# Banded attention weights built on TensorE from sixteen diagonal blocks, and tanh written over its own input

## The chip, the cores and the metric

The kernel runs on all 8 cores of one Trainium2 chip. Every core runs the same program on its own batch element (2048 tokens of width 1024); nothing passes between the cores. The metric is the device time in microseconds of the slowest core.

## The reference

For each of 8 batch elements, `x` is `[2048, 1024]` in f32, and two layers follow, each with a layer norm ahead of it, a layer norm behind it, and a residual:

```python
xn     = layernorm(x)
q      = xn @ w1
proj   = pad(xn) @ w2                         # 7 zero rows ahead, 8 behind
score[t, k] = tanh(proj[t + k] + q[t]) @ v    # k = 0..15
weight = softmax(score, axis=-1)              # 16 weights per token
out[t] = sum_k weight[t, k] * pad(xn)[t + k]
x      = x + layernorm(out)

h      = layernorm(x)                          # mixture of 8 experts, top 2, and one shared
y      = sum_e cw[e] * (silu(h @ wg[e]) * (h @ wu[e])) @ wd[e] + shared(h)
x      = x + layernorm(y)
```

The change lies in the first layer alone.

## The kernel before, in words

Every engine has one list of operations, written in program order by `P.add(engine, fn, waits, inc)`. An engine works through its list strictly in that order; an operation waits for the semaphore values named in `waits`, and `inc` raises a semaphore when it is done. So the order in which the Python code calls `P.add` sets the order of work on each engine.

**The attention layer.** 16 tiles of 128 tokens are taken in 4 stages (`sp`) of 4 tiles (512 tokens).

- `emit_windows_qproj(sp)` copies the last part of the window along, transposes the new tiles of `xn` on TensorE into `xnw` (`ptw`, L300 and L308), then computes q (8 groups of 8 matmuls into `pq`, L320, each evicted to `qw` by VectorE, L329) and the local projection (8 groups of 8+8 matmuls into `pq` and `ptf`, L339 and L346, evicted to `pjw`, L356 and L359). `pq` has two banks.
- `emit_scores_softmax(sp)` is a loop of 32 steps (16 offsets k times two halves of the width). Each step is: four VectorE additions into one of two buffers `argb[i]` (L388, 128x512 each), one tanh on ScalarE of the whole 128x2048 buffer into `tanb[i]` (L394), and four matmuls with `vsp` that add the result into 16 rows of one PSUM bank `psc` (L403). The additions wait for the tanh that read this `argb[i]` two steps ago; the tanh waits for the matmuls that read this `tanb[i]` two steps ago. Behind the loop come a copy of the scores (L414), a burst of 12 matmuls on `idb` and `argb` whose result nobody reads (`warm_burst`, L604), four small transposes (L419) and the softmax into `wts`.
- `make_tail(sp, ev_wt)` gives a list of thunks that finish the stage: for each of the 4 tiles `t_ub` builds `uwide`, a 128x384 band matrix with `weight[t, k]` on diagonal `121 + k`; `t_band_tr` transposes its two or three 128x128 pieces on TensorE (`ptb`, L490) and copies them to `wtb` (L499); `t_band` multiplies them with `xn` into the two banks `pB` (L514); `t_stats` takes the statistics (L534) and moves `pB` to `bbuf` (L550). Behind the four tiles come one `t_rstd` and four `t_x2`, which normalise (ScalarE, L568) and add to `x2` (VectorE, L577).

The thunks of stage `sp` are pumped one by one into the code of stage `sp+1`: one after each window transpose, q group and projection group, and what is left after each step of the score loop. The thunks of the last stage have nothing beside them. So 12 of the 16 calls of `t_ub` stand between transposes and projection groups of the next stage, and 4 stand alone.

`t_ub` before is VectorE work only: one memset of `uwide` (L464) and 16 `scalar_tensor_tensor` operations (L470), each adding `idb * wts[:, k]` to a shifted 128x128 piece of `uwide`. Since neighbouring pieces overlap, each waits (`drain`) until the one ahead of it has been written.

**The expert layer** (from L610 on) waits for all of the attention layer: its weight loads on the GpSimd queue wait for `bar`, the last semaphore values of TensorE, VectorE and ScalarE, and its matmuls need the finished `x2`. It is not touched.

**Start.** Constants and `w1`, `w2` are loaded by the GpSimd queue in the order `idb`, `onesb`, `vsp`, `wrt`, `w1s`, `w2s`.

Of the kernel before, what the change touches and what calls it, by code (L numbers as in the profile page):

```python
# [10 lines left out]
BF16 = mybir.dt.bfloat16  # L11
# [5 lines left out]
KW = 16  # L17
# [66 lines left out]
def build_program(cfg: Cfg):  # L84
    nc = bass.Bass("TRN2", target_bir_lowering=False)
# [15 lines left out]
    d_iw = nc.dram_tensor("iw", [128, 448], F32, kind="ExternalInput").ap()  # L101
# [4 lines left out]
    with ExitStack() as ctx:  # L106
        en = ctx.enter_context
# [4 lines left out]
        P = Prog(sems)  # L112

        x2 = en(nc.sbuf_tensor("x2", [128, TT * H], F32))
        idf = en(nc.sbuf_tensor("idf", [128, 128], F32))
        idb = en(nc.sbuf_tensor("idb", [128, 128], BF16))
        onesb = en(nc.sbuf_tensor("onesb", [128, 128], BF16))
        vsp = en(nc.sbuf_tensor("vspb", [128, HC * KW * KW], BF16))
# [11 lines left out]
        for q in range(4):  # L130
# [3 lines left out]
                out=x2[:, lo * H: hi * H],  # L134
                in_=d_x.rearrange("(tt p) h -> p tt h", p=128)[:, lo:hi, :]),
                inc=f"dx{q}", inc_amt=16))
        ev_x = ev_xq[-1]
        ev_id = P.add("sync", lambda e: e.dma_start(out=idf[:], in_=d_id),
                      inc="dc", inc_amt=16)
        P.add("gpsimd", lambda e: e.dma_start(out=idb[:], in_=d_id),  # L140
              inc="dgc", inc_amt=16)
        P.add("gpsimd", lambda e: e.dma_start(out=onesb[:], in_=d_ones),
              inc="dgc", inc_amt=16)
        P.add("gpsimd", lambda e: e.dma_start(
            out=vsp[:], in_=d_vsp.rearrange("(c p) j -> p c j", p=128)),
            inc="dgc", inc_amt=16)
        ev_const = P.add("gpsimd", lambda e: e.dma_start(
            out=wrt[:], in_=d_wrt.rearrange("(c p) j -> p c j", p=128)),
            inc="dgc", inc_amt=16)
        ev_iw = ev_idb = ev_onesb = ev_vsp = ev_wrt = ev_const  # L150
# [34 lines left out]
        with ExitStack() as actx:  # L185
            aen = actx.enter_context
# [5 lines left out]
            pjw = aen(nc.sbuf_tensor("pjw", [128, HC * 768], BF16))  # L192
            GW = min(4, HC)
            argb = [aen(nc.sbuf_tensor(f"argb{i}", [128, GW * 512], BF16)) for i in range(2)]
            tanb = [aen(nc.sbuf_tensor(f"tanb{i}", [128, GW * 512], BF16)) for i in range(2)]
            scf = aen(nc.sbuf_tensor("scf", [16, 512], F32))
            sct = aen(nc.sbuf_tensor("sct", [128, 64], F32))
            wts = aen(nc.sbuf_tensor("wts", [128, 4 * KW], F32))
            uwide = [aen(nc.sbuf_tensor(f"uwide{i}", [128, 384], BF16)) for i in range(2)]
# [8 lines left out]
            pB = [aen(nc.psum_tensor(f"pB{i}", [128, 512], F32)) for i in range(2)]  # L208

            P.add("gpsimd", lambda e: e.dma_start(  # L210
                out=w1s[:], in_=d_w1.rearrange("(c p) j -> p c j", p=128)),
                inc="dw", inc_amt=16)
            ev_w2 = P.add("gpsimd", lambda e: e.dma_start(
                out=w2s[:], in_=d_w2.rearrange("(c p) j -> p c j", p=128)),
                inc="dw", inc_amt=16)
# [9 lines left out]
            for tau in range(TT):  # L225
# [4 lines left out]
                    waits=[ev_a1], inc="s")  # L230
# [7 lines left out]
            ev_pB_free = [None, None]  # L238
            ev_sc_prev = None
            argb_free = [None, None]  # L240
            tanb_free = [None, None]
            uw_free = [None, None]
# [2 lines left out]
            ev_s_sct = None  # L245
            ev_s_smx = None
            ev_s_bbuf = None
            zscr_free = [None]
            ev_q = ev_pj = None
            ev_sctv = None  # L250
# [117 lines left out]
            def emit_scores_softmax(sp, pump=None):  # L368
                nonlocal ev_sc_prev, ev_s_sct, ev_s_smx, ev_sctv, ev_tf_last
                ev_q_sp, ev_pj_sp = ev_q, ev_pj  # L370
# [10 lines left out]
                for k in range(KW):  # L381
                    for cq in range(HC // GW):
                        i = nq % 2
                        eva = None
                        for ci in range(GW):
                            c = cq * GW + ci
                            eva = P.add("vector", lambda e, k=k, c=c, ci=ci, i=i:
                                        e.tensor_tensor(  # L388
                                argb[i][:, ci * 512:(ci + 1) * 512],
                                pjw[:, c * 768 + 121 + k: c * 768 + 121 + k + 512],  # L390
                                qw[:, c * 512:(c + 1) * 512], op=A.add),
                                waits=[ev_q_sp, ev_pj_sp, argb_free[i]],
                                inc="v" if ci == GW - 1 else None)
                        evth = P.add("scalar", lambda e, i=i: e.activation(  # L394
                            tanb[i][:], argb[i][:], AF.Tanh),
                            waits=[eva, tanb_free[i]], inc="s")
                        argb_free[i] = evth
                        for ci in range(GW):
                            c = cq * GW + ci
                            ev_sc = P.add("tensor", lambda e, k=k, c=c, ci=ci, i=i,  # L400
                                          first=(nq == 0 and ci == 0),
                                          last=(nq == NQ - 1 and ci == GW - 1):
                                          e.matmul(  # L403
                                psc[0:16, 0:512],
                                vsp[:, c * KW * KW + k * KW:
                                    c * KW * KW + (k + 1) * KW],
                                tanb[i][:, ci * 512:(ci + 1) * 512],
                                start=first, stop=last),
                                waits=[evth, ev_vsp, ev_sc_prev],
                                inc="t" if ci == GW - 1 else None)  # L410
                        tanb_free[i] = ev_sc
                        nq += 1
                        spp(1)
# [4 lines left out]
                for blk in range(4):  # L418
# [3 lines left out]
                        waits=[ev_scev, ev_id, ev_tf_last, ev_ptf_tail], inc="t")  # L422
# [13 lines left out]
                for blk in range(4):  # L436
# [5 lines left out]
                        waits=[evn], inc="s")  # L442
# [5 lines left out]
                ev_wt = None  # L448
# [8 lines left out]
            def make_tail(sp, ev_wt):  # L457
                b0 = sp * 4
                state = {"ev_v2": None, "ev_bev": [None] * 4}

                def t_ub(blk, ui):
                    def f():
                        def ub(e, blk=blk, ui=ui):
                            e.memset(uwide[ui][:], 0.0)  # L464
                            last = None
                            for k in range(KW):
                                off = k + 121
                                wcol = wts[:, blk * KW + k: blk * KW + k + 1]
                                e.drain()
                                last = e.scalar_tensor_tensor(  # L470
                                    uwide[ui][:, off: off + 128], idb[:], wcol,
                                    uwide[ui][:, off: off + 128],
                                    op0=A.mult, op1=A.add)
                            return last
                        state[f"ub{blk}"] = P.add(
                            "vector", ub, waits=[ev_wt, ev_idb, uw_free[ui]],
                            inc="v")
                        P.drain("vector")
                    return f

                def t_band_tr(blk, tau, kaps, ui):
# [104 lines left out]
                for blk in range(4):  # L586
                    tau = b0 + blk
                    kaps = [kp for kp in (tau - 1, tau, tau + 1) if 0 <= kp < TT]
                    ui = blk % 2
# [26 lines left out]
            for sp in range(NSP):  # L616
                ev_wt = emit_scores_softmax(sp, pump=tail)
# [10 lines left out]
        with ExitStack() as mctx:  # L628
# [226 lines left out]
            for th in range(2):  # L855
# [6 lines left out]
                for ei in range(NE):  # L862
# [6 lines left out]
                    for ic in range(IC):  # L869
                        sl = nload % 3  # L870
                        gn, un = gname[ic % 2], uname[ic % 2]
                        gb, ub = pbank[gn], pbank[un]
# [266 lines left out]
```

How the kernel before makes its waits and increments, by code:

```python
            def body(eng):  # L68
                for fn, wl, inc in ops[engname]:
                    for semname, val in wl:
                        eng.wait_ge(sems[semname], val)
                    if fn is None:
                        continue
                    inst = fn(eng)
                    if inc is not None:
                        inst.then_inc(sems[inc[0]], inc[1])
```

## Time and profile before

| what | us |
|---|---|
| median of the runs before (2 runs, 3165.08 and 3167.39) | 3166.24 |
| the profiled execution, its own time | 3169.17 |
| span of its slowest core (core 5), first to last instruction | 3167.4 |
| spans of the 8 cores | 3153.4 to 3167.4 |
| attention layer on core 5, to the last addition to `x2` | 0 to 816.7 |
| expert layer on core 5 | 816.7 to 3167.4 |

The span is what the trace shows; the execution's own time holds 1.8 us more around it. Rows of the trace are in us from the start of the span. A timeline row is: start, duration, engine, line, operation, what it writes and reads, how many instructions are merged, and in brackets how long the engine stood idle before it and who released it. TensorE's matmuls are pipelined and their ends are modelled. "PEclk" is the clock that TensorE was granted: 1.00 is 2.4 GHz, 0.50 is 1.2 GHz.

### The profile page before, as it was taken

The numbers are of one execution on the slowest core, as the hardware profiler recorded it, in microseconds if no ns is written. First come the engines' busy times: TensorE is split into PE (matmuls) and PEld (weight loads), VectorE is DVE, ScalarE is ACT, GpSimd is POOL, SyncE is SP. The second block draws the span as 40 slices with busy tenths as digits, with TensorE's granted clock in tenths as the row PEclk, the third lists the DMA queues.
The fourth block names the chain that finished last, engine by engine and source line by source line (L and its number), as shares of the span: only waits on it lengthen the run. The fifth ranks groups of instructions, "written<-read, shape, count | busy, mean of one in ns | idle before, by whom it ended". The sixth has DMA issues, their size and how long they took to land.

```text
span 3167.4 us, 31804 instructions; the slowest of 8 cores (3153.4 to 3167.4 us)
## 1 busy us (share of the span) xinstructions
PE 2518.9 (80%) x11570; PEld 1122.3 (35%) x11570; DVE 1213.6 (38%) x2370; ACT 539.8 (17%) x485; POOL 505.3 (16%) x550
## 2 busy tenths in 40 slices
PE   2654554633267999999999999599999999999995
PEld 1221221201123444444444444244444444444442
DVE  5564655556434233233233222522222232222225
ACT  2522517053211111101111101010010010010010
POOL 0000000000012222212212312022222222222220
PEclk9986887767579999999999999699999999999997
DMA  7000000000247776966966967478768778769763
GB/s 168 1 0 1 1 1 1 1 0 0 20 39 71 67 66 63 92 62 64 90 62 64 91 65 68 83 67 83 73 65 83 73 66 84 72 65 86 73 65 72
DMA packets 626055, 179.41 MB, mean 57 GB/s; under 512 B 618608, under 2 KB 619760, under 8 KB 625904
## 3 DMA queue, kind: packets, MB, share of 16 engines
q0 software_dynamic: 621344, 160.55, 53.9%
q1 hardware_dynamic: 4560, 16.84, 1.5%
q8 instruction: 95, 1.56, 0.2%
q14 instruction: 56, 0.46, 0.1%
HBM read 329.48 MB, written 8.39 MB: 107 GB/s over the span
## 4 chain that ended last, share of the span: by engine, by line
PE 72%; DVE 14%; ACT 8%; issue 3%; DVEq 2%; DMA 2%; ACTq 0%; POOLq 0%
PE py L983 21%; PE pg L893 12%; PE pu L909 12%; PE py L909 10%; PE py L893 10%; ACT tanb L394 6%; DVE uwide L470 3%; PE pq L320 2%; PE pq L339 1%; DVE bnb L154 1%; DVEq L62 1%; DVE argb L388 1%; PE psc L403 1%; DMA wdb<-wd 1%; PE pB L514 1%
## 5 line engine op out<-in xcount | busy, mean ns | idle before, releaser
L983 PE MATMUL py<-hpr,wdb 128*128 128x512 bf16 x3168 | 713.4, 387 | 48.4 <-DVE hpr L932 40.1
L983 PEld LDWEIGHTS py<-hpr,wdb 128*128 128x128 bf16 x3168 | 312.8, 100 | 438.4 <-issue 88.7
L893 PE MATMUL pg<-xm_fm,wgb 128*128 128x512 bf16 x1728 | 395.1, 382 | 3.0 <-DVE cwb L841 3.0
L909 PE MATMUL pu<-xm_fm,wub 128*128 128x512 bf16 x1728 | 390.6, 379 | 0.0
L879 POOL DMA_DIRECT2D wgb<-wg x176 | 156.2, 887 | 1400.3 <-DVE x L577 810.9
L924 DVE TENSOR_TENSOR t1b<-sgb,pu 128x1024 bf16<-128x1024 bf16 x108 | 131.9, 1221 | 527.4 <-PE pu L909 527.4
L1001 DVE SCALAR_TENSOR_TENSOR yfm<-py,yfm 128x1024 f32<-128x1024 f32 x128 | 156.8, 1225 | 456.7 <-PE py L983 447.9
L909 PE MATMUL py<-xm_fm,wub 128*128 128x512 bf16 x1440 | 325.5, 379 | 0.0
L893 PE MATMUL py<-xm_fm,wgb 128*128 128x512 bf16 x1440 | 325.5, 379 | 0.0
L403 PE MATMUL psc<-tanb,vspb 128*16 128x512 bf16 x512 | 155.7, 434 | 188.3 <-ACT tanb L394 188.3
L394 ACT ACTIVATE tanb<-argb 128x2048 bf16<-128x2048 bf16 x128 | 233.8, 1897 | 330.7 <-DVE argb L388 308.6
L920 ACT ACTIVATE sgb<-pg 128x1024 bf16<-128x1024 f32 x108 | 110.6, 1024 | 991.2 <-PE pg L893 991.1
L924 DVE TENSOR_TENSOR t1b<-sgb,py 128x1024 bf16<-128x1024 bf16 x90 | 109.9, 1221 | 436.7 <-PE py L909 436.7
L893 PEld LDWEIGHTS pg<-xm_fm,wgb 128*128 128x128 bf16 x1728 | 170.0, 98 | 210.3 <-issue 9.4
L909 PEld LDWEIGHTS pu<-xm_fm,wub 128*128 128x128 bf16 x1728 | 169.1, 98 | 203.9
L883 POOL DMA_DIRECT2D wub<-wu x176 | 155.7, 884 | 331.8 <-PE py L909 166.5
L893 PEld LDWEIGHTS py<-xm_fm,wgb 128*128 128x128 bf16 x1440 | 140.9, 98 | 169.9
L909 PEld LDWEIGHTS py<-xm_fm,wub 128*128 128x128 bf16 x1440 | 140.9, 98 | 169.9
L388 DVE TENSOR_TENSOR argb<-pjw,qw 128x512 bf16<-128x512 bf16 x512 | 182.6, 420 | 45.2 <-ACT tanb L394 42.3
L973 POOL DMA_DIRECT2D wdb<-wd x80 | 84.8, 1060 | 686.0 <-PE pg L833 383.6
L920 ACT ACTIVATE sgb<-py 128x1024 bf16<-128x1024 f32 x90 | 92.2, 1024 | 520.7 <-PE py L893 520.7
L403 PEld LDWEIGHTS psc<-tanb,vspb 128*16 128x16 bf16 x512 | 40.7, 93 | 300.9 <-issue 275.9
(119 smaller groups left out, 1318.8 us busy)
## 6 DMA issues: line engine op xcount, KB each, us to landing
wgb<-wg POOLq DMA_DIRECT2D x176, 256.0 KB, 5.3
wub<-wu POOLq DMA_DIRECT2D x176, 256.0 KB, 5.3
wdb<-wd POOLq DMA_DIRECT2D x128, 352.0 KB, 6.6
x<-x SPq DMA_DIRECT2D x4, 2048.0 KB, 24.3
out<-osc SPq DMA_DIRECT2D x16, 512.0 KB, 2.6
wgb<-wgs POOLq DMA_DIRECT2D x22, 256.0 KB, 4.9
wub<-wus POOLq DMA_DIRECT2D x22, 256.0 KB, 5.3
wdb<-wds POOLq DMA_DIRECT2D x16, 352.0 KB, 6.3
```

What stands on the lines that cost most here:

```text
L388: e.tensor_tensor(argb[i][:, ci * 512:(ci + 1) * 512], pjw[:, c * 768 + 121 + k: c * 768 + 121 + k + 512], qw[:, c * 512:(c + 1) * 512], o ...
L394: evth = P.add("scalar", lambda e, i=i: e.activation(tanb[i][:], argb[i][:], AF.Tanh), waits=[eva, tanb_free[i]], inc="s")
L403: e.matmul(psc[0:16, 0:512], vsp[:, c * KW * KW + k * KW: c * KW * KW + (k + 1) * KW], tanb[i][:, ci * 512:(ci + 1) * 512], start=first, s ...
L470: last = e.scalar_tensor_tensor(uwide[ui][:, off: off + 128], idb[:], wcol, uwide[ui][:, off: off + 128], op0=A.mult, op1=A.add)
L879: evlg_ = P.add("gpsimd", lambda e, sl=sl, src_g=src_g: e.dma_start(out=wgb[sl][:], in_=src_g.rearrange("(c p) j -> p c j", p=128)), waits ...
L883: evlu_ = P.add("gpsimd", lambda e, sl=sl, src_u=src_u: e.dma_start(out=wub[sl][:], in_=src_u.rearrange("(c p) j -> p c j", p=128)), waits ...
L893: last = e.matmul(gb[:, gg * 512:(gg + 1) * 512], wgb[sl][:, c * 128:(c + 1) * 128], xm_fm[:, c * T + tof + gg * 512: c * T + tof + (gg + ...
L909: last = e.matmul(ub[:, gg * 512:(gg + 1) * 512], wub[sl][:, c * 128:(c + 1) * 128], xm_fm[:, c * T + tof + gg * 512: c * T + tof + (gg + ...
L920: evsg = P.add("scalar", lambda e, gb=gb: e.activation(sgb[:], gb[:, 0:TH], AF.Silu), waits=[evg, ev_sgb_cons], inc="s")
L924: evt1 = P.add("vector", lambda e, ub=ub: e.tensor_tensor(t1b[:], sgb[:], ub[:, 0:TH], op=A.mult), waits=[evsg, evu, ev_t1b_cons], inc="v")
L983: last = e.matmul(pbank[pyn][:, gg * 512:(gg + 1) * 512], wdb[sl][:, ic * 128:(ic + 1) * 128], hpr[:, ic * TH + gg * 512: ic * TH + (gg + ...
L1001: e.scalar_tensor_tensor(yfm[:, c * TH:(c + 1) * TH], pbank[pyn][:, 0:TH], 1.0, yfm[:, c * TH:(c + 1) * TH], op0=A.mult, op1=A.add),
```

## The change

Two things are changed, both in the attention layer.

1. `tanb` becomes another name for `argb`: the tanh writes over its own input. The additions of a step therefore wait for two things: the tanh that used the buffer two steps ago, as before, and the four matmuls that read its result.
2. `t_ub` no longer adds up the band on VectorE. VectorE writes 16 separate diagonal blocks into a new buffer `DallA` (128x2048), TensorE multiplies each with a shifted piece of a constant `iwb` (448 columns, ones on diagonal `p + 160`) and adds all 16 products up in `pB[0]`, and VectorE copies 384 columns from there to `uwide`. `pB[0]` has to be free before (the copy to `bbuf` of the tile ahead), and `DallA` too (the matmuls of the tile ahead). One more constant load, `iwb`, stands first in the GpSimd queue.

```diff
+        iwb = en(nc.sbuf_tensor("iwb", [128, 448], BF16))
...
+        P.add("gpsimd", lambda e: e.dma_start(out=iwb[:], in_=d_iw),
+              inc="dgc", inc_amt=16)
         P.add("gpsimd", lambda e: e.dma_start(out=idb[:], in_=d_id),
               inc="dgc", inc_amt=16)
...
-            tanb = [aen(nc.sbuf_tensor(f"tanb{i}", [128, GW * 512], BF16)) for i in range(2)]
+            tanb = argb
+            DallA = aen(nc.sbuf_tensor("DallA", [128, KW * 128], BF16))
...
-                                waits=[ev_q_sp, ev_pj_sp, argb_free[i]],
+                                waits=[ev_q_sp, ev_pj_sp, argb_free[i],
+                                       tanb_free[i]],
                                 inc="v" if ci == GW - 1 else None)
...
-                        def ub(e, blk=blk, ui=ui):
-                            e.memset(uwide[ui][:], 0.0)
+                        nonlocal ev_dallA_free
+
+                        def dbuild(e, blk=blk):
                             last = None
                             for k in range(KW):
-                                off = k + 121
                                 wcol = wts[:, blk * KW + k: blk * KW + k + 1]
-                                e.drain()
-                                last = e.scalar_tensor_tensor(
-                                    uwide[ui][:, off: off + 128], idb[:], wcol,
-                                    uwide[ui][:, off: off + 128],
-                                    op0=A.mult, op1=A.add)
+                                last = e.tensor_scalar(
+                                    DallA[:, k * 128:(k + 1) * 128], idb[:],
+                                    wcol, None, op0=A.mult)
                             return last
-                        state[f"ub{blk}"] = P.add(
-                            "vector", ub, waits=[ev_wt, ev_idb, uw_free[ui]],
-                            inc="v")
+                        evd = P.add("vector", dbuild,
+                                    waits=[ev_wt, ev_idb, ev_dallA_free],
+                                    inc="v")
                         P.drain("vector")
+
+                        def ummA(e):
+                            last = None
+                            for k in range(KW):
+                                s0_ = 39 - k
+                                last = e.matmul(
+                                    pB[0][:, 0:384],
+                                    DallA[:, k * 128:(k + 1) * 128],
+                                    iwb[:, s0_: s0_ + 384],
+                                    start=(k == 0), stop=(k == KW - 1))
+                            return last
+                        evm = P.add("tensor", ummA,
+                                    waits=[evd, ev_iw, ev_pB_free[0]], inc="t")
+                        ev_dallA_free = evm
+                        ev = P.add("vector", lambda e, ui=ui: e.tensor_copy(
+                            uwide[ui][:], pB[0][:, 0:384]),
+                            waits=[evm, uw_free[ui]], inc="v")
+                        ev_pB_free[0] = ev
+                        state[f"ub{blk}"] = ev
```

On TensorE, in the q projection of the second stage around its second tile, the program before has these rows (`pq` with `w1s` is a q group, `ptb` the transposes of the band, `pB` its product with `xn`):

```order
L320 MATMUL pq<-xnw,w1s 128x512 x24
L490 MATMUL ptb<-idb,uwide 128x128 x3
L320 MATMUL pq<-xnw,w1s 128x512 x8
L514 MATMUL pB<-xn,wtb 128x512 x2
L320 MATMUL pq<-xnw,w1s 128x512 x8
```

and the changed program these (its line numbers are higher by 5 to 23):

```order
L325 MATMUL pq<-xnw,w1s 128x512 x16
L488 MATMUL pB<-iwb,DallA 128x384 x16
L325 MATMUL pq<-xnw,w1s 128x512 x8
L513 MATMUL ptb<-idb,uwide 128x128 x3
L325 MATMUL pq<-xnw,w1s 128x512 x8
L537 MATMUL pB<-xn,wtb 128x512 x2
```

The 16 new matmuls stand one q group ahead of the transposes, so the third group of eight that used to stand ahead of the tile's TensorE work now stands behind the new matmuls.

On VectorE at the same place, before (`qw` is the eviction of a q group):

```order
L550 COPY bbuf<-pB 128x512 x2
L329 CAST qw<-pq 128x512
L464 MEMSET uwide 128x384
L470 SCALAR_TENSOR_TENSOR uwide<-idb,wts,uwide 128x128 x16
L329 CAST qw<-pq 128x512
L499 COPY wtb<-ptb 128x384
```

and in the changed program:

```order
L573 COPY bbuf<-pB 128x512 x2
L334 CAST qw<-pq 128x512
L475 TENSOR_SCALAR DallA<-idb,wts 128x128 x16
L497 CAST uwide<-pB 128x384
L334 CAST qw<-pq 128x512
L522 COPY wtb<-ptb 128x384
```

The copy of `uwide`, which waits for TensorE, stands directly behind the 16 products, ahead of the next eviction.

On VectorE at the third step of the score loop of the first stage, before and then in the changed program (what an operation waits for in brackets, s is ScalarE's semaphore, t TensorE's):

```order
L388 TENSOR_TENSOR argb<-pjw,qw 128x512 [waits s]
```

```order
L393 TENSOR_TENSOR argb<-pjw,qw 128x512 [waits s,t]
```

The additions of a step now wait for TensorE too.

## Rows read from the trace of the kernel before

**Rows 1.** The page's chain that ended last: share of the span by engine.

```profile
PE 72%; DVE 14%; ACT 8%; issue 3%; DVEq 2%; DMA 2%; ACTq 0%; POOLq 0%
```

**Rows 2.** Stretches: length, busy of PE, PEld, DVE, ACT, POOL (count), PEclk, DMA, GB/s.

```profile
118.70:177.00 58.30, 33.24 (x124) 9.39 (x124) 42.93 (x120) 57.81 (x32) 0.00 (x0) 0.95 0.00 1
319.05:362.90 43.85, 25.61 (x92) 7.11 (x92) 32.68 (x92) 43.44 (x24) 0.00 (x0) 0.92 0.00 0
504.33:546.30 41.97, 24.13 (x88) 6.71 (x88) 31.25 (x88) 41.62 (x23) 0.00 (x0) 0.93 0.00 1
695.37:735.50 40.13, 23.13 (x84) 6.42 (x84) 29.81 (x84) 39.82 (x22) 0.00 (x0) 0.92 0.00 1
```

**Rows 3.** Timeline, score loop of the first stage: tanh, matmuls and additions of one step.

```profile
122.82 54.11 ACT L394 ACTIVATE tanb<-argb 128x2048 bf16<-128x2048 bf16 x30 [0.42 <-PE psc L403]
...
126.67 1.02 PE L403 MATMUL psc<-tanb,vspb 128*16 128x512 bf16 x4 [0.78 <-ACT tanb L394]
128.43 1.43 DVE L388 TENSOR_TENSOR argb<-pjw,qw 128x512 bf16<-128x512 bf16 x4 [0.37 <-ACT tanb L394]
```

**Rows 4.** Timeline, one step of the second stage's loop with a `t_x2` beside it.

```profile
299.35 1.43 DVE L388 TENSOR_TENSOR argb<-pjw,qw 128x512 bf16<-128x512 bf16 x4
300.93 1.91 ACT L394 ACTIVATE tanb<-argb 128x2048 bf16<-128x2048 bf16 x1 [3.00 <-DVE argb L388]
...
302.98 1.87 PE L403 MATMUL psc<-tanb,vspb 128*16 128x512 bf16 x4 [4.17 <-ACT tanb L394]
...
305.39 1.43 DVE L388 TENSOR_TENSOR argb<-pjw,qw 128x512 bf16<-128x512 bf16 x4
```

**Rows 5.** Timeline, end of the first score loop: last matmuls, copy, burst.

```profile
177.07 1.02 PE L403 MATMUL psc<-tanb,vspb 128*16 128x512 bf16 x4 [0.78 <-ACT tanb L394]
178.20 0.68 DVE L414 COPY scf<-psc 16x512 f32<-16x512 f32 x1 [3.34 <-PE psc L403]
...
179.03 2.75 PE L604 MATMUL psc<-argb,idb 128*128 128x512 bf16 x12 [0.93 <-DVE scf L414]
```

**Rows 6.** Granted clock: a stretch (columns as in rows 2), then timeline rows of matmuls.

```profile
288.00:320.00 32.00, 9.33 (x20) 1.98 (x20) 13.67 (x31) 17.54 (x13) 0.00 (x0) 0.50 0.00 1
```

```profile
256.38 1.89 PE L339 MATMUL pq<-xnw,w2s 128*128 128x512 bf16 x8 [1.14 <-DVE pjw L359]
...
260.76 3.17 PE L339 MATMUL pq<-xnw,w2s 128*128 128x512 bf16 x8 [2.04 <-DVE pjw L359]
```

**Rows 7.** Timeline, start of the third stage's loop: third tanh.

```profile
462.75 1.91 ACT L394 ACTIVATE tanb<-argb 128x2048 bf16<-128x2048 bf16 x1 [0.42 <-PE psc L403]
```

**Rows 8.** Groups by form, 0 to 1100 us: count, busy, mean ns, idle before.

```profile
L470 DVE SCALAR_TENSOR_TENSOR uwide<-idb,wts,uwide 128x128 bf16<-128x128 bf16 x256 | 90.4, 353 | 20.1 <-issue 1.4
...
L329 DVE CAST qw<-pq 128x512 bf16<-128x512 f32 x32 | 22.1, 692 | 43.9 <-PE pq L320 40.3 <-PE pB L514 2.5 <-issue 1.1
...
L359 DVE CAST pjw<-ptf 128x128 bf16<-128x128 f32 x32 | 9.0, 280 | 0.0
```

**Rows 9.** Timeline, expert layer: eight products of `idb` with one column.

```profile
898.76 1.39 DVE L817 TENSOR_SCALAR Dsc<-idb,cw_all 128x128 bf16<-128x128 bf16 x8 [0.17 <-DVE cw_all L778]
```

**Rows 10.** Timeline, second tile's `t_ub` in the second stage's q projection.

```profile
209.69 0.38 DVE L464 MEMSET uwide<- 128x384 bf16 x1
210.14 6.77 DVE L470 SCALAR_TENSOR_TENSOR uwide<-idb,wts,uwide 128x128 bf16<-128x128 bf16 x16
...
217.05 0.48 PE L490 MATMUL ptb<-idb,uwide 128*128 128x128 bf16 x3 [8.92 <-DVE uwide L470]
...
217.32 3.34 PE L320 MATMUL pq<-xnw,w1s 128*128 128x512 bf16 x8
```

**Rows 11.** Timeline, last stage's tail, second tile: the band's product on TensorE.

```profile
768.20 2.72 PE L514 MATMUL pB<-xn,wtb 128*128 128x512 bf16 x6 [0.61 <-DVE wtb L499]
```

**Rows 12.** DMA issues, 0 to 300 us: KB, us to landing; and the first user of the weights.

```profile
w2s<-w POOLq DMA_DIRECT2D x1, 2048.0 KB, 58.3
```

```profile
71.60 1.87 PE L320 MATMUL pq<-xnw,w1s 128*128 128x512 bf16 x4 [0.94 <-DVE xnw L308]
```

More of the change, by code:

```diff
@@ L247, in build_program @@
             ev_s_bbuf = None
+            ev_dallA_free = None
             zscr_free = [None]
```

## Prediction

> **What bounds the kernel now.** I read the views from the whole to the place. The chain that ended last [rows 1] is 72% TensorE; that is the expert layer, which the change does not touch and which starts only when the attention layer is complete. So whatever the attention layer gains or loses is passed on one to one: the weight loads of the expert layer wait for its end too. Inside the attention layer two stretches matter.
>
> The first is the score loop. In the table of stretches [rows 2] I cut out the parts of the four loops in which nothing else is mixed in: 32, 24, 23 and 22 tanh in 58.3, 43.9, 42.0 and 40.1 us, 101 of the 128 steps. In each of the four rows ScalarE is busy for 99% of the stretch. The timeline [rows 3] gives the beat: 30 tanh in 54.11 us, 1.80 us each; the four matmuls take 1.02 and then idle 0.78, the additions take 1.43 and idle 0.37. ScalarE sets the end; the two others have room. The other 27 steps have tail work beside them and a longer beat (299.35 to 305.39 is 6.04 us [rows 4]).
>
> The second is `t_ub`, 16 times. In the second tile of the second stage [rows 10] VectorE works from 209.69 to 216.91 (7.22 us), and TensorE stands still for 8.92 us before the transposes of the band at 217.05.
>
> **The tanh in place.** The buffer of a step may be rewritten only when its matmuls are done. Before, additions and matmuls of neighbouring steps lay beside each other; now one buffer goes round a closed circle, and there are two buffers. The circle from rows: additions 1.43; to the tanh 0.15 (300.78 to 300.93); tanh 1.91; to the matmuls 0.14 (302.84 to 302.98) [rows 4]; matmuls; from their end back to VectorE 0.11 (178.09 to 178.20) [rows 5]. Without the matmuls that is 3.74. The matmuls take 1.02 at full clock [rows 3] and 1.87 at half clock [rows 4]. So a circle is 4.76 or 5.61 us and carries two steps, which took 3.60 before: 1.16 or 2.01 us more per pair. The third and every later step of a stretch waits this way: 15, 11, 11 and 10 circles in the stretches of 32, 24, 23 and 22, 47 in all. That gives +54.5 us at full clock and +94.5 at half clock. The loosely filled steps (6.04 apart, matmuls done 0.54 before the next additions [rows 4]) have slack and cost nothing.
>
> Which clock? In the loop before, the matmuls are busy 57% with gaps of 0.78 and the clock in rows 2 is 0.92 to 0.95 (the first matmuls of each are slow, the rest fast). In the stretch 288 to 320 they are busy 29% and the clock is 0.50 throughout [rows 6]. The new loop at full clock would be busy 43% and has gaps of 0.78 and 1.94 in turn, between the two. A gap of 2.04 us was enough once: eight matmuls took 1.89 at 256.38 and 3.17 at 260.76 behind that gap [rows 6]. And once the clock is lost the new loop is busy 1.87 of 2.80 us, with gaps, where the rises in this trace came out of almost unbroken work. I take three quarters of the way to half clock: +84.5.
>
> The Trainium skill ("TensorE: Matmul & The Clock Gate", § HAM oscillation — how this bites in real kernels) ties the loss of the clock to long idle gaps only, longer than any in the new loop; by that the loop would stay at full clock. The same page's § A second HAM failure mode: psum-queue depth-cycling says that short idles between groups of matmuls make the clock swing between both levels, which is nearer to my mix. The gap of 2.04 us agrees with the second. No row shows 43%.
>
> Two small terms go with it. If the loop ends at half clock, the burst of 12 matmuls, 2.75 us at full clock [rows 5] and ahead of the score transposes on TensorE, takes up to 5.3: I take +1.5 for each of four, +6 (0 to +10). And at the start of the third and fourth loop the third additions, which before were written ahead so that only the tanh waited for TensorE, at 462.75 [rows 7], wait for it themselves; additions and hand-over (1.43+0.15) then stand between: +1.5 each, +3 (0 to +4).
>
> **The band on TensorE.** Removed: 7.22 us of VectorE per tile, 16 x 353 ns plus drains [rows 8] and a memset. Added on VectorE: 16 products like those of L817. Eight take 1.39 us [rows 9], so sixteen at most 2.78. Then 0.13 to TensorE. 16 matmuls of 384 columns are as many columns as 12 of 512: 2.75 us at full clock [rows 5], and with 0.427 us per 512 columns (eight in 3.57 or 3.34, the rows at half clock) 5.28 at half. TensorE has stood idle there for most of the 8.92 us of before [rows 10] and starts at half clock; the rise comes during or just behind them: I take 4.9. Then 0.11, and the copy of 384 columns from PSUM: between 280 ns for 128 and 692 for 512 [rows 8] that is 555 ns, and 0.12 on. Together 2.78+0.13+4.9+0.11+0.56 = 8.48 against 7.22: +1.26 per tile (-0.9 to +1.6). VectorE is free for longer but can't use it: the copy of `uwide` stands directly behind the products, and the next evictions behind it.
>
> For the 12 tiles among projections two things come on top. One group of eight matmuls (1.9, with the 128-column ones 2.3) that used to run while VectorE was busy now stands behind the new matmuls, with the 0.67 of the copy hidden beside it: +1.6. And what follows runs at full clock, 1.7 instead of 3.34 at 217.32 [rows 10]: -1.6. So +1.26 per tile, +15 in all. Bounds: every new matmul at full clock and the gain kept, -0.9 per tile, -11; all at half clock and no gain, +3.2, +38. For the four tiles of the last stage the six matmuls behind, 2.72 at 768.20 [rows 11], fall to about 1.45: -1.3 against +1.26, so 0 (-6 to +6).
>
> The new constant load costs nothing: `w2s` lands about 64 us (issued at 5.4, 58.3 on the way [rows 12]), its first user starts at 71.60 behind VectorE's copies. The extra load moves 0.2 MB ahead of it and some 0.9 us of issue; the cover is 7 us.
>
> **Sum.** +84.5 + 6 + 3 + 15 + 0 = +108.5 us, 3.4%. On the profiled execution's 3169.2 that is 3277.7; the median of the runs is 2.9 lower, so 3275.
>
> **The rivals.**
> - *The loop keeps full clock.* +54.5, burst 0, starts +3, band about +10: +67, 3234. For it: gaps of 0.78 to 1.94 are shorter than most idles after which the clock was gone. Against it: 43% busy and the 2.04 gap. Its lower bound, with the band at -11, is 3210.
> - *The lost clock is everywhere.* +94.5, burst +10, starts +4, band +38, tail +6: +152.5, 3319. For it: TensorE is idle ahead of every group in the attention layer. Against it: the 16 new matmuls are the kind of unbroken work after which the clock rose.
> - *The band pays for the loop.* VectorE saves 7.22 - 3.34 = 3.88 us per tile, 62 us in 16. If all of that came off the path while the loop kept full clock, 54.5 - 62 = -7.5: 3159, not slower. It decides from the point where TensorE's 16 matmuls are hidden beside VectorE work, so that only 3.3 us per tile are left on the path. Against it: 2.75 us is their least, and the copy behind them is next in VectorE's order.
> - *The new wait never binds*, because the matmuls are done when the additions come up. The trace excludes it: the additions at 128.43 start before the matmuls of the tanh for which they wait, at 126.67 + 1.80 = 128.47, which then last 1.02 [rows 3].
>
> **How the numbers follow.** My forecast 0.58, full clock in the loop 0.22, half clock everywhere 0.16, band pays 0.04. A measurement of this kernel tells about 2% (63 us) from no change. The border is 3229.6; below it lie the third rival and the lower part of the first: within 2% 0.17, faster 0.02, slower 0.81. The range 3222 to 3312 reaches from the lower middle of the first rival to just short of the second.
>
> **What would show it right or wrong.** In the changed profile: the beat of the tanh in the unmixed loops 2.4 to 2.8 instead of 1.80, VectorE idle before the additions and released by the matmuls, ScalarE busy about 70% there; the granted clock there tells which circle it is. The 16 products 2.7 us together, the 16 new matmuls 2.8 to 5.3, the copy 0.55. The four stages start later by 25 to 35 us each, and the expert layer has the same length as before. A beat of 1.80 would prove the main step wrong; a beat right and a total under 3220 would mean that the band gains what I hold for hidden.

## The result, and the profile after

The changed kernel takes 3.5% longer: ratio of the runs 1.0353, 95% interval 1.0337 to 1.0368, that is 112 us on 3166; the forecast was 109. Its profiled execution took 3277.57 us with a span of 3275.1 on the slowest core (core 3). These comparisons leave out executions in which the cores of a die ran at a lower clock and the time is longer whatever the kernel; the plain medians over all runs (3279.88 and 3256.6) mix them in and say little, and where some cores of a profiled execution below still show it, the others are given as well.

Where it lies shows best at the moment of the first weight load of the expert layer, which waits for the whole attention layer. Averaged over the 8 cores it stands at 816.3 us in the kernel before and at 925.8 in the changed one, +109.5; from there to the end it is 2344.1 and 2344.7 us. The expert layer passes the loss on and adds nothing. The average over the cores is used below as "the attention layer", since single cores of one execution lie 5 us apart at that point in the kernel before and up to 19 in one of the experiments (`e4_filler`).

The stretches of the changed kernel (core 3): first the four unmixed parts of the score loops (the counterparts of rows 2), then what follows each of them up to the next loop or the end of the layer. Columns: length, busy time of TensorE, its weight loads, VectorE, ScalarE, GpSimd, each with its count, granted clock, DMA share, GB/s.

```profile
119.50:207.60 88.10, 56.81 (x124) 11.96 (x124) 43.08 (x121) 60.95 (x33) 0.00 (x0) 0.52 0.00 0
354.10:418.50 64.40, 38.90 (x92) 8.60 (x92) 32.73 (x92) 45.50 (x24) 0.00 (x0) 0.61 0.00 1
567.50:630.40 62.90, 39.98 (x88) 8.45 (x88) 31.36 (x88) 43.70 (x23) 0.00 (x0) 0.53 0.00 1
784.50:844.40 59.90, 38.13 (x84) 8.08 (x84) 29.93 (x84) 41.57 (x22) 0.00 (x0) 0.53 0.00 0
207.60:309.60 102.00, 64.89 (x337) 30.84 (x337) 44.50 (x162) 1.27 (x8) 0.00 (x0) 0.83 0.00 1
418.50:521.30 102.80, 66.41 (x338) 31.73 (x338) 44.54 (x162) 1.27 (x8) 0.00 (x0) 0.81 0.00 1
630.40:731.70 101.30, 66.10 (x327) 31.09 (x327) 44.58 (x167) 1.28 (x9) 0.00 (x0) 0.80 0.00 0
844.40:926.00 81.60, 32.29 (x117) 12.98 (x117) 34.22 (x120) 7.72 (x14) 0.00 (x0) 0.67 0.00 0
```

Against [rows 2] the same 32, 24, 23 and 22 steps take 88.1, 64.4, 62.9 and 59.9 us instead of 58.3, 43.9, 42.0 and 40.1. ScalarE is busy for 69 to 71% instead of 99%, VectorE for about half. No engine is busy all the time any more; and the granted clock is 0.52 to 0.61 instead of 0.92 to 0.95, so TensorE's 124 recorded matmuls of the first loop need 56.8 us instead of 33.2. Together the loops are some 91 us longer. For the second half of the table the kernel before has 98.4, 95.8, 97.0 and 81.2 us (last tanh to first tanh or last addition to `x2`), the changed one 102.1, 102.9, 101.4 and 82.1: +16.

One circle of the first loop, from the timeline of the changed kernel (the counterpart of rows 3):

```profile
138.31 1.91 ACT L400 ACTIVATE argb<-argb 128x2048 bf16<-128x2048 bf16 x1 [0.74 <-DVE argb L393]
139.69 1.43 DVE L393 TENSOR_TENSOR argb<-pjw,qw 128x512 bf16<-128x512 bf16 x4 [1.53 <-PE psc L409]
140.36 1.86 PE L409 MATMUL psc<-argb,vspb 128*16 128x512 bf16 x4 [0.78 <-ACT argb L400]
...
142.33 1.43 DVE L393 TENSOR_TENSOR argb<-pjw,qw 128x512 bf16<-128x512 bf16 x4 [1.21 <-PE psc L409]
...
143.92 1.91 ACT L400 ACTIVATE argb<-argb 128x2048 bf16<-128x2048 bf16 x1 [0.74 <-DVE argb L393]
```

The tanh on one buffer starts at 138.31, its matmuls at 140.36, their end releases the additions at 142.33, and those the next tanh on that buffer at 143.92: 5.61 us for two steps, the forecast circle at half clock to the hundredth. The loop did not hold the full clock when it had it. It starts at half clock; four matmuls behind a gap of 2.03 us ran at full clock, the next four did not, and from 130 us to the end of the loop the granted clock is 0.50:

```profile
127.35 1.02 PE L409 MATMUL psc<-argb,vspb 128*16 128x512 bf16 x4 [2.03 <-ACT argb L400]
129.15 1.87 PE L409 MATMUL psc<-argb,vspb 128*16 128x512 bf16 x4 [0.78 <-ACT argb L400]
```

Who waited for whom between 119 and 208 us (engine, line, waited for: total, times, longest) has a line that the kernel before did not have at all:

```profile
DVE argb L393 <- PE psc L409: 42.9, 30, 4.2
```

Behind the loops, the burst (before: 2.75 us in all four stages, rows 5) and the second tile of the second stage (rows 10):

```profile
210.51 4.70 PE L627 MATMUL psc<-argb,idb 128*128 128x512 bf16 x12 [0.93 <-DVE scf L420]
...
847.31 5.28 PE L627 MATMUL psc<-argb,idb 128*128 128x512 bf16 x12 [0.93 <-DVE scf L420]
```

```profile
243.13 2.68 DVE L475 TENSOR_SCALAR DallA<-idb,wts 128x128 bf16<-128x128 bf16 x16
245.96 4.05 PE L488 MATMUL pB<-iwb,DallA 128*128 128x384 bf16 x16 [6.00 <-DVE DallA L475]
249.85 1.89 PE L325 MATMUL pq<-xnw,w1s 128*128 128x512 bf16 x8
250.12 0.56 DVE L497 CAST uwide<-pB 128x384 bf16<-128x384 f32 x1 [4.31 <-PE pB L488]
251.58 0.33 PE L513 MATMUL ptb<-idb,uwide 128*128 128x128 bf16 x3
251.75 1.89 PE L325 MATMUL pq<-xnw,w1s 128*128 128x512 bf16 x8
```

The sixteen products take 2.68 us instead of the 7.22 of before; but the transposes of the band start 8.45 us behind the first product (before 7.36), because the new matmuls and the q group behind them stand between on TensorE; the copy to `uwide`, for which VectorE idles 4.31 us, is done at 250.68 already. What follows runs at full clock: 1.89 for the eight matmuls at 251.75 against 3.34 at 217.32.

### The profile page after: what moved, and what is told of

It reads as the page before. It is cut to its first block, busy times and chain, and to the rows that moved or that the text cites. A ratio compares the mean times of both kernels' runs of the same rounds, so it can differ in the third digit from the quotient of the medians.

```text
span 3275.1 us, 32197 instructions; the slowest of 8 cores (3265.8 to 3275.1 us)
## 1 busy us (share of the span) xinstructions
PE 2640.6 (81%) x11826; PEld 1155.9 (35%) x11826; DVE 1168.3 (36%) x2370; ACT 548.9 (17%) x485; POOL 505.9 (15%) x551
## 3 DMA queue, kind: packets, MB, share of 16 engines
q8 instruction: 97, 1.59, 0.2%
## 4 chain that ended last, share of the span: by engine, by line
PE 74%; DVE 13%; ACT 6%; issue 3%; DMA 2%; DVEq 1%; ACTq 0%; SPq 0%; POOLq 0%
PE py L1006 20%; PE pg L916 12%; PE pu L932 11%; PE py L932 9%; PE py L916 9%; ACT argb L400 4%; PE psc L409 3%; DVE argb L393 3%; PE pB L488 2%; PE pq L325 2%; PE pq L344 2%; DVE DallA L475 1%; DMA x<-x 1%; DVEq L62 1%; DMA wdb<-wd 1%
## 5 line engine op out<-in xcount | busy, mean ns | idle before, releaser
L409 PE MATMUL psc<-argb,vspb 128*16 128x512 bf16 x512 | 226.9, 595 | 205.1 <-ACT argb L400 205.1
L400 ACT ACTIVATE argb<-argb 128x2048 bf16<-128x2048 bf16 x128 | 242.9, 1908 | 420.4 <-DVE argb L393 404.1
L409 PEld LDWEIGHTS psc<-argb,vspb 128*16 128x16 bf16 x512 | 48.6, 109 | 379.9 <-issue 376.8
```

The source lines that it names most:

```text
L400: evth = P.add("scalar", lambda e, i=i: e.activation(tanb[i][:], argb[i][:], AF.Tanh), waits=[eva, tanb_free[i]], inc="s")
L409: e.matmul(psc[0:16, 0:512], vsp[:, c * KW * KW + k * KW: c * KW * KW + (k + 1) * KW], tanb[i][:, ci * 512:(ci + 1) * 512], start=first, s ...
```

## The experiments

Seven kernels, in two groups, each group on one chip beside the kernel before. Theory: the loss is the closed circle of the in-place buffers with its matmuls at half clock, and the band on TensorE costs little. "The attention layer" is the average over the cores, as above. A loop is counted from the start of its first tanh to the end of its last; a stretch between loops is what lies behind it up to the next first tanh.

**The first part alone.** The kernel before with

```diff
-            tanb = [aen(nc.sbuf_tensor(f"tanb{i}", [128, GW * 512], BF16)) for i in range(2)]
+            tanb = argb
...
-                                waits=[ev_q_sp, ev_pj_sp, argb_free[i]],
+                                waits=[ev_q_sp, ev_pj_sp, argb_free[i],
+                                       tanb_free[i]],
```

> The kernel before with the first part alone: tanh in place, the band still on VectorE. Theory (the closed circle at half clock): the beat in the unmixed loops is 2.80 us, granted clock there near 0.5, total about 90 to 100 us above the kernel before (3260). Rival (the time was lost because the new matmuls of the band disturb the loops): no more than 20 us above before, beat 1.80.

Measured: 3273.75 us, ratio 1.0334 (1.0314 to 1.0354); attention layer 923.1, +106.8, a little above the expected 90 to 100. The first loop, as above:

```profile
119.50:207.70 88.20, 56.80 (x124) 11.92 (x124) 43.22 (x121) 61.10 (x33) 0.00 (x0) 0.52 0.00 0
```

The line is that of the whole change to within 0.2 us. The rival (the band disturbs the loops) falls: there is no band on TensorE here.

**Only the wait.** The kernel before with its four buffers and the second half of that diff, `tanb_free[i]` added to the waits, and nothing else.

> The kernel before, tanb and argb four buffers as they were, with nothing but the added wait: the additions of a step wait for the matmuls of two steps ago. Theory (the wait closes the circle, sharing the memory has no part): the same as e1_inplace_only, beat 2.75 to 2.80, total 3273. Rival (the shared memory slows the tanh or the additions): faster than e1_inplace_only by 20 us or more.

Measured (two executions): 3273.66 us, ratio 1.0325 (1.0301 to 1.0349); attention layer 923.4. Its first loop:

```profile
119.50:207.70 88.20, 56.81 (x124) 11.99 (x124) 43.67 (x123) 61.12 (x33) 0.00 (x0) 0.52 0.00 0
```

Sharing the bytes costs nothing that can be measured (0.3 us between the two); the wait that sharing brings costs everything.

**The second part alone.** The changed kernel with `tanb` of its own and without the added wait. SBUF is too small for that as it stands, so `DallA` lies in the bytes of `zscr` and `uwide` in those of `scf`, whose uses don't overlap in time:

```diff
+            zscr = [aen(nc.sbuf_tensor("zscr0", [128, H], F32))] * 2
+            DallA = zscr[0][:, :].bitcast(BF16)
...
+            scfu = aen(nc.sbuf_tensor("scfu", [128, 512], F32))
+            scf = scfu[0:16, :]
+            uwide = [scfu[:, :].bitcast(BF16)[:, i * 384:(i + 1) * 384] for i in range(2)]
```

> The second part alone: the band on TensorE, tanb a buffer of its own again. To make room, DallA lies in the bytes of zscr and uwide in those of scf. Theory: loops at 1.80 us per step and full clock as before; the stretches between the loops 3 to 5 us longer each and the last tail equal, total +10 to +15 us against before (3177). Rival (band pays, the freed VectorE time comes off the path): 30 to 60 us below before.

Measured: ratio 1.0008 (0.9997 to 1.0019); attention layer 822.1, +5.8; the expert layer happened to be 2.5 shorter (2341.6). The loops are as before:

```profile
119.80:178.00 58.20, 33.24 (x124) 9.34 (x124) 42.99 (x120) 57.77 (x32) 0.00 (x0) 0.95 0.00 1
```

Averaged over the cores, the three stretches between the loops are 8.0 us longer together, and the tail behind the last loop is 2.3 shorter. (On core 5, from which the row above comes, they are longer by 1.4, 3.0 and 4.1 and the tail is equal; but its granted clock from 550 to 650 us is 0.78, where core 0 has 0.83, and over the span cores 4 to 7 have 0.91 and cores 0 to 3 have 0.92; on these the attention layer ends at 820.1, +4.) So the band is neither a gain nor much of a loss; the rival of 30 to 60 us saved falls, and the expected +10 to +15 was too much. The parts add up within 3 us: 106.8 + 5.8 = 112.6 against 109.5 for both.

**Three buffers.** The changed kernel, in place, with three buffers in turn (`uwide` lies in the bytes of `scf` for room).

```diff
-            argb = [... for i in range(2)]
+            argb = [... for i in range(3)]
...
-                        i = nq % 2
+                        i = nq % 3
```

> The changed kernel with three in-place buffers in turn instead of two (uwide in the bytes of scf for room). Theory (closed circle of additions, tanh and matmuls, divided by the number of buffers): 5.61/3 = 1.87 at half clock, then ScalarE's 1.80 is nearly the bound again and the clock rises as before; beat 1.80, total 80 to 95 us below the changed kernel (3188). Rival (writing in place itself slows ScalarE or VectorE, by sharing the buffer's memory): beat stays over 2.3 and the total within 20 us of the changed kernel.

Measured: ratio 1.0021 (1.0008 to 1.0033) against the kernel before; attention layer 821.6, 104 us less than with two buffers, more than the 80 to 95 expected. First loop and three rows of its timeline:

```profile
118.20:176.20 58.00, 34.14 (x124) 9.45 (x124) 42.82 (x120) 57.79 (x32) 0.00 (x0) 0.94 0.00 1
```

```profile
138.31 9.10 ACT L401 ACTIVATE argb<-argb 128x2048 bf16<-128x2048 bf16 x5
139.68 1.43 DVE L394 TENSOR_TENSOR argb<-pjw,qw 128x512 bf16<-128x512 bf16 x4 [0.37 <-PE psc L410]
140.35 1.02 PE L410 MATMUL psc<-argb,vspb 128*16 128x512 bf16 x4 [0.78 <-ACT argb L401]
```

Tanh in place, one every 1.80 us (9.10 for five), with full clock, and the additions idle 0.37 as before. The work of a circle is as long as ever, but three steps share it: 4.76/3 = 1.59, below ScalarE's 1.80. The additions do wait for TensorE now (those at 139.68 for matmuls that ran from 138.55 to 139.57), but they are done at 141.11, and the tanh that reads them starts only at 141.91, when ScalarE comes free.

**Filler for the clock.** The changed kernel with three matmuls without a reader behind each step's four:

```diff
+            def filler(e):
+                last = None
+                for _ in range(3):
+                    last = e.matmul(pq[0][:, 0:512], idb[:], xnw[:, 0:512],
+                                    start=True, stop=True)
+                return last
...
                         tanb_free[i] = ev_sc
+                        P.add("tensor", filler)
```

> The changed kernel with three matmuls of 512 columns whose result nobody reads behind the four of each step of the score loop, to keep TensorE busier. Theory (the beat contains the matmuls at half clock, 1.87 instead of 1.02): the granted clock in the loops rises to 1.00, the circle is 4.76 and the beat 2.38, total about 40 us below the changed kernel (3238). Rival (the clock has no part in it, TensorE is simply given more work): the clock stays at 0.5, a step's matmuls take 3.0 us, the beat grows to 3.0 or more and the total rises by 10 to 60 us.

Measured: ratio 1.0249 (1.0195 to 1.0302), attention layer 893.4, 32 us less than in the changed kernel though TensorE does 384 matmuls more. On cores 4 to 7 the granted clock of this execution was lower (0.90 to 0.91 over the span, against 0.92 on the others); cores 0 to 3 alone give 886.5, 39 us less, and the one execution in which all eight cores kept 0.92 took 3237.11 us, 41 less than the changed kernel's 3278. First loop on core 5, and the larger part of the second on core 0:

```profile
119.30:196.50 77.20, 56.96 (x217) 15.97 (x217) 43.04 (x120) 60.91 (x33) 0.00 (x0) 0.96 0.00 0
350.00:398.00 48.00, 35.55 (x141) 10.13 (x140) 28.01 (x79) 38.55 (x21) 0.00 (x0) 1.00 0.00 1
```

In the first loop the clock is 0.96 and 32 steps take 77.2 us; 15 circles of 4.76 instead of 5.61 should save 12.8, and 88.1 - 77.2 = 10.9. In the second loop of core 0 the clock is 0.50 from 325 to 345 us and 1.00 from 355 on, and a circle there takes 4.76 (two tanh on one buffer start at 350.97 and 355.73). On cores 0 to 3 the loops together are 25 us shorter than in the changed kernel and what lies between and behind them 14. So the theory stands, and its size of 40 as well. The rest of the circle remains: even at full clock the first loop is 19 us longer than the 58.3 of before.

**Fewer new matmuls.** `e2_band_only` with one of the 16 new matmuls per tile; the other 15 are left out, so most of the band is missing from what is computed.

```diff
-                            for k in range(KW):
+                            for k in range(1):
```

> e2_band_only with one of the 16 new matmuls per tile; 15 are left out, so the output is not the reference's. Theory (the new matmuls stand on the path of every tile at 4 to 5 us): the attention layer is 40 to 65 us shorter than in e2_band_only. Rival (they run beside VectorE's work, which is why the band part cost so little): less than 15 us shorter.

Measured: ratio 0.986 (0.9837 to 0.9883); attention layer 778.1, 44 us less than in `e2_band_only`: 2.75 us per tile. The new matmuls do stand on the path. But the sixteen take 4.73 us on average, and one takes 0.47, so 4.26 us fewer on TensorE bring 2.75 back; what is lost again shows in the product behind them in the last tail, first `e6_one_matmul`, then `e2_band_only`:

```profile
746.07 2.70 PE L537 MATMUL pB<-xn,wtb 128*128 128x512 bf16 x6 [0.61 <-DVE wtb L522]
```

```profile
773.33 4.93 PE L488 MATMUL pB<-iwb,zscr 128*128 128x384 bf16 x16 [6.46 <-DVE zscr L475]
779.08 0.33 PE L513 MATMUL ptb<-idb,scfu 128*128 128x128 bf16 x3 [0.81 <-DVE scfu L497]
780.02 1.46 PE L537 MATMUL pB<-xn,wtb 128*128 128x512 bf16 x6 [0.61 <-DVE wtb L522]
```

The long new work brings the clock up for what follows it, 1.46 instead of 2.70; without it that work runs at half clock. The expected 40 to 65 was met at its lower end.

**A version that beats both.** The band comes out of TensorE already transposed: the shifted identity is the stationary operand and a diagonal block the moving one, for those pieces only that a block reaches (31 matmuls of 128 columns per tile). The copy to `uwide` and the transposes go; `wtb` is copied from `pB[0]`. `tanb` is separate.

```diff
-                            for k in range(KW):
-                                s0_ = 39 - k
-                                last = e.matmul(
-                                    pB[0][:, 0:384],
-                                    DallA[:, k * 128:(k + 1) * 128],
-                                    iwb[:, s0_: s0_ + 384],
-                                    start=(k == 0), stop=(k == KW - 1))
+                            for ki, kp in enumerate(kaps):
+                                m = kp - tau + 1
+                                ks = [k for k in range(KW)
+                                      if (m != 0 or k < 7) and (m != 2 or k > 7)]
+                                for k in ks:
+                                    s0_ = 39 - k + 128 * m
+                                    last = e.matmul(
+                                        pB[0][:, ki * 128:(ki + 1) * 128],
+                                        iwb[:, s0_: s0_ + 128],
+                                        DallA[:, k * 128:(k + 1) * 128],
+                                        start=(k == ks[0]), stop=(k == ks[-1]))
```

> As e2_band_only (tanb of its own, DallA in the bytes of zscr), but TensorE writes the band already transposed: the shifted identity is the stationary operand, the 128 columns of each product the moving one, only for the pieces a product reaches (31 matmuls of 128 columns instead of 16 of 384), so the copy to uwide and the transposes fall away. Theory (what counts of the band is the chain VectorE products, matmuls, copies): per tile 0.56 and 0.12 for the copy and 0.3 to 0.5 for the transposes go, and the matmuls take 2.2 to 3.7 us instead of 4.05 to 5.3; 2 us less in each of 16 tiles, 25 to 35 us below e2_band_only, 20 to 30 below the kernel before (3140). Rival (128-column matmuls with a weight load each are no faster, and the stages between the loops are bound by the projection groups and evictions): within 8 us of e2_band_only.

Measured: 3141.07 us, ratio 0.9912 (0.9894 to 0.9931) against the kernel before: the fastest of those that compute the whole result. Attention layer 798.3, 18 less than before and 24 less than `e2_band_only`. Cores 0 to 3, two of them above all, had a lower granted clock in this execution (0.90 to 0.91 over the span); cores 4 to 7 give 794.0, 22 less than before, and 26 less than cores 0 to 3 of `e2_band_only`. One tile of the last tail:

```profile
755.26 2.69 DVE L473 TENSOR_SCALAR zscr<-idb,wts 128x128 bf16<-128x128 bf16 x16
758.10 3.47 PE L490 MATMUL pB<-zscr,iwb 128*128 128x128 bf16 x31 [6.46 <-DVE zscr L473]
761.67 0.56 DVE L506 CAST wtb<-pB 128x384 bf16<-128x384 f32 x1 [3.72 <-PE pB L490]
762.37 2.72 PE L521 MATMUL pB<-xn,wtb 128*128 128x512 bf16 x6 [0.81 <-DVE wtb L506]
```

From the first product to the band's own product it is now 7.11 us; in `e2_band_only` it was 9.5 (the matmuls at 773.33 start 2.84 behind the first product, the product at 780.02). Per tile that is 1.5 to 1.6 us on average instead of the expected 2: the shorter work no longer brings the clock up in this tile (2.72 instead of 1.46). The rival (no gain from small matmuls) falls.

## Why the prediction's total held, and which of its steps failed

- **Total and direction.** Forecast 3275 and +108.5; measured 112 by the ratio and 109.5 in the attention layer. That it hit so closely is luck: the losses in and around the loops were put too low by about as much as the loss of the band was put too high.
- **The closed circle.** Right, and shown by three runs: the wait alone brings it (+107.1), a third buffer removes it (-104), and its length at half clock, 5.61, stands in the timeline. 47 circles were counted; the loops grew by 91 us, 1.94 per circle, against the 2.01 of pure half clock.
- **The clock in the loop.** The term was too small: "three quarters of the way to half clock", +84.5. The measured place is about nine tenths of the way (91 between 54.5 and 94.5), with granted clocks of 0.52, 0.61, 0.53 and 0.53. By the long-idle rule of the Trainium skill ("TensorE: Matmul & The Clock Gate", § HAM oscillation — how this bites in real kernels) the loop, with gaps of 0.8 to 2.0 us, would have kept full clock; the trace says otherwise. The section behind it (§ A second HAM failure mode: psum-queue depth-cycling), on short idles, is nearer, but what the traces show is mostly a clock that stays low, not one that swings. `e4_filler` shows that the clock and not the matmuls as such makes up this part: more work, less time.
- **Burst and loop starts.** +6 and +3 forecast. The bursts took 4.70, 5.08, 4.94 and 5.28 instead of 2.75, +9 in all; the parts of the later loops in front of the unmixed stretches grew by 0.8, 0.5 and 0.8, +2. With the loops that makes 102, and `e1_inplace_only` has 106.8; the rest, some 5 us between and behind the loops, is in no term, and no run separates it.
- **The band among the projections: the step that failed.** +15 forecast. The three stretches between the loops are longer by 8.0 us in `e2_band_only` against the kernel before, and by 4.2 in the changed kernel against `e1_inplace_only`. What was wrong is the working per tile. From the first product to the transposes of the band it has 10.1 us, the chain of 8.48 and 1.6 for the group of matmuls behind it. The changed kernel takes 9.15 on average, 8.45 to 10.10, in 11 of the 12 tiles (7.41 before; the twelfth, the last of the third stage, takes 14.54 and took 13.15). So a tile loses 1.7 there and not 2.9. The group was put at 2.3 us including the copy beside it; it costs 1.73 where it is a q group, as at 249.85 to 251.58, 2.2 where it is a projection group, and in the first tile of each stage no such group stands there, only eight window transposes. In the tile shown the new matmuls were short as well, 4.05 against the 4.9 taken; on average over the 16 tiles they took 4.73. The gain behind them was put at -1.6; in the tile shown it is 3.34 - 1.89 = 1.45.
- **The last tail.** 0 forecast. `e2_band_only` is 2.3 us shorter there than the kernel before, and the changed kernel 1.4 shorter than `e1_inplace_only`, inside the stated -6 to +6 and by the mechanism named: 4.1 to 5.3 us of matmuls, and 1.46 instead of 2.72 behind them.
- **The constant load** shifted the first tanh by 0.9 us at most (119.6 against 118.7 on the slowest cores; averaged over the cores it comes 0.6 earlier than before), so nothing can be put down to it.
- **The rivals.** "Full clock" and "the band pays" fall by the table of stretches and by `e2_band_only`. "Half clock everywhere" had the loop right and the band wrong: the new matmuls raise the clock for their neighbours.

## What to carry to other kernels

A buffer written in place joins the waits of its readers to those of its writer: add up the whole circle (here additions 1.43, tanh 1.91, matmuls 1.87, hand-overs 0.40) and divide it by the number of buffers; only if the quotient stays under the slowest engine's beat is the saved memory free. Three buffers of one kind were as good here as two of each and took a quarter less memory. When a change makes TensorE wait in a circle as here, price it at half clock too, since the circle itself then grows (4.76 to 5.61); and when work is moved to TensorE, count also what it does to the clock of the work behind it and which work then stands behind it.

## What was not expected of the hardware

The granted clock stayed at 0.50 for 77 us (130 to 207.6) in a loop in which TensorE was busy for 64% of the time (56.81 of 88.10 us), while in the kernel before the same matmuls, busy for 57%, had 0.95 over the loop; three buffers and the filler put it back to 0.94 and 0.96. With two buffers the slower level lengthens the very circle in which TensorE waits. Whether that is what keeps it low is not shown: it was at full clock once, at 127.35, and lost it within one group of matmuls. 31 matmuls of 128 columns with a weight load each took 3.47 us at half clock, 0.11 each, about the same time per column as the wide ones.
